# Row sums of a softmax: from the exponential's accumulator to a column of ones beside the values

## The reference

```python
x = x + attn(layernorm(x));  x = x + ffn(layernorm(x))

# attn, B=4, S=1024, D=128
scores = einsum('bqe,bke->bqk', x @ W_qk, x) * D**-0.5 + (kpos - qpos) * slope
attn   = softmax(where(qpos >= kpos, scores, -inf), axis=-1)
out    = einsum('bqk,bkd->bqd', attn, x @ W_v.T)

# ffn, HIDDEN=384, weights int32 / 127
out = (silu(x @ wg.T) * (x @ wu.T)) @ wd.T
```

## Time and profile before

| | us |
|---|---|
| median of 3 runs | 144.62 |
| lowest and highest run | 144.57, 145.28 |
| the profiled execution's own time | 145.67 |
| its span, first to last instruction | 143.9 |
| opening (weights, first projections), up to about | 24 |
| four rounds of attention, up to about | 104 |
| FFN, up to the end | 143.9 |

### The profile page before, as it was taken

The page is one execution under the profiler, slowest core; times in us unless marked ns, Lnnn a source line. Parts: engine busy times, 40 slices in busy tenths (PEclk is TensorE's granted clock), DMA queues, the critical chain, the costliest instruction groups (busy, mean ns, idle before and its releaser), DMA issues.

```text
span 143.9 us, 3450 instructions
## 1 busy us (share of the span) xinstructions
PE 122.8 (85%) x1215; PEld 91.9 (64%) x1215; DVE 120.7 (84%) x341; ACT 110.7 (77%) x251; POOL 97.6 (68%) x157
## 2 busy tenths in 40 slices
PE   0239658999999999999999998979998899999942
PEld 0028345867987769978779776657755656675541
DVE  0729989998697996969996969999879999988781
ACT  4034588999976999949999769985699978999830
POOL 6490769964993454992438943798999999646810
PEclk9999999999999999999999999999999999999995
DMA  4997000000000000000000000000000222022204
GB/s 129 221 244 190 0 0 2 7 2 0 5 0 0 5 0 2 5 0 0 0 5 0 5 0 2 2 5 0 5 0 0 77 77 66 12 73 77 77 0 146
DMA packets 9811, 5.18 MB, mean 36 GB/s; under 512 B 448, under 2 KB 9792, under 8 KB 9792
## 3 DMA queue, kind: packets, MB, share of 16 engines
q1 hardware_dynamic: 9792, 4.92, 12.2%
HBM read 2.82 MB, written 2.10 MB: 34 GB/s over the span
## 4 chain that ended last, share of the span: by engine, by line
PE 50%; DVE 23%; ACT 9%; POOL 7%; DMA 4%; issue 3%; SPq 2%; DVEq 0%
PE work_ps L556 7%; POOL hidden_lo L411 6%; PE attn_ps L571 5%; PE attn_ps L573 4%; PE attn_ps L572 4%; PE score_ps L504 4%; PE score_ps L506 4%; DVE probsT_lo L824 4%; PE score_ps L505 4%; DMA wd_int<-in_L_ffn_w_down_dram 4%; DVE biased L841 3%; PE score_ps L595 2%; PE score_ps L592 2%; DVE stats L726 2%; ACT silu L1069 2%
## 5 line engine op out<-in xcount | busy, mean ns | idle before, releaser
L571 PE MATMUL attn_ps<-v_hi,probsT_hi 128*128 128x128 f16 x144 | 25.8, 219 | 3.0 <-DVE xs L851 2.4
L824 DVE TENSOR_TENSOR probsT_lo<-work_ps,probsT_hi 128x512 f16<-128x512 f32 (+3 forms) x48 | 25.2, 552 | 3.5 <-ACT probsT_hi L1007 3.4
L1007 ACT CAST probsT_hi<-work_ps 128x512 f16<-128x512 f32 (+3 forms) x48 | 21.4, 484 | 7.7 <-PE work_ps L556 7.4
L992 ACT ACTIVATE probs<-biased,neg_max 128x128 f32<-128x128 f32 (+7 forms) x32 | 25.0, 783 | 1.9 <-DVE neg_max L841 1.9
L841 DVE CUSTOM_DVE_ANT_0 biased<-score_ps,bias,neg_score_scale 128x128 f32<-128x128 f32 (+7 forms) x32 | 25.8, 806 | 0.6 <-PE score_ps L506 0.6
L573 PE MATMUL attn_ps<-v_hi,probsT_lo 128*128 128x128 f16 x144 | 25.8, 219 | 0.0
L572 PE MATMUL attn_ps<-v_lo,probsT_hi 128*128 128x128 f16 x144 | 25.8, 219 | 0.0
L556 PE MATMUL work_ps<-ident,probs 128*128 128x128 f32 x144 | 21.4, 274 | 0.2 <-DVE probsT_lo L824 0.2
L411 POOL TENSOR_TENSOR hidden_lo<-hidden,hidden_hi 128x512 f16<-128x512 f32 x13 | 17.6, 1375 | 5.1 <-ACT hidden_hi L1075 5.1
L556 PEld LDWEIGHTS work_ps<-ident,probs 128*128 128x128 f32 x144 | 16.5, 141 | 3.2 <-DVE probsT_lo L824 0.5
L437 POOL TENSOR_TENSOR xT_lo<-whole,xT_hi 128x512 f16<-128x512 f32 x8 | 9.3, 1163 | 13.6 <-ACT whole L986 13.6
(11 more groups left out here) (135 smaller groups left out, 346.7 us busy)
## 6 DMA issues: line engine op xcount, KB each, us to landing
out_dram<-xs SPq DMA_DIRECT2D x7, 256.0 KB, 2.7
xs<-in_L_attn_x_dram SPq DMA_DIRECT2D x3, 512.0 KB, 7.4
xs<-in_L_attn_x_dram SPq DMA_DIRECT2D x2, 256.0 KB, 3.0
out_dram<-xs SPq DMA_DIRECT2D x2, 128.0 KB, 1.9
wgu_int<-in_L_ffn_w_gate_dram SPq DMA_DIRECT2D x1, 192.0 KB, 3.1
wgu_int<-in_L_ffn_w_up_dram SPq DMA_DIRECT2D x1, 192.0 KB, 3.4
wd_int<-in_L_ffn_w_down_dram SPq DMA_DIRECT2D x1, 192.0 KB, 5.1
wqk_in<-in_L_attn_W_qk_dram SPq DMA_DIRECT2D x1, 64.0 KB, 2.9
```

The costliest lines, as they stand in the source:

```text
L571: pe.matmul(attn_ps[:, 0:D], p_hi, v_j, start=(j == 0), stop=False)
L824: dve.tensor_tensor(probsT_lo[:, i % 2, cols], work_ps[:, bank, 0:n], probsT_hi[:, i % 2, cols], ALU.subtract).then_inc(work_emptied, 1)
L992: act.activation(probs[:, i % 2, 0:n], biased[:, i % 2, 0:n], ACT.Exp, bias=neg_max[:, i:i + 1], scale=-1.0, accum_out=prob_sum[:, i:i + 1 ...
L1007: act.copy(probsT_hi[:, i % 2, CW * h:CW * h + n], work_ps[:, bank, 0:n]).then_inc(probsT_hi_ready, 1)
```

## The change

What it does, part by part (line numbers of the changed kernel are lower by some 35 to 40):

- The exponential has no `accum_out`. `scale_sum`, with its instruction on ScalarE for every tile, is gone, and so is `prob_sum`.
- The values' high half is laid out as eight tiles of 136 columns (`VW = D + 8`), of which column 128 holds 1.0. GpSimd writes these ones once in the opening; TensorE waits for `v_ones_ready` once.
- In `weigh_values` the two products with the values' high half have 129 columns, so that column 128 of `attn_ps` becomes the sum of the row's probabilities, high and low part. The product with the values' low half keeps 128.
- VectorE multiplies that column by `wpow_inv` (a `tensor_scalar` from PSUM), inverts it and adds, all in `add_attention`. Each of the three waits for the semaphore of the one before, and the first for `attn_ready`. The reciprocal at the head of a tile is gone; its waits for scores and probabilities now stand before `bias_scores`.
- `place`, `emptied`, `copied_before` and their like are replaced by one list, `ring`, of everything that goes through `work_ps` in order; it gives the same banks and the same counts. Tests of the kind `isinstance(b, int)` go.

```diff
-        prob_sum = sb("prob_sum", [P, TB], F32)
-        v_hi = sb("v_hi", [P, 2, S], F16)
-        v_lo = sb("v_lo", [P, 2, S], F16)
+        VW = D + 8
+        v_hi = sb("v_hi", [P, 2, TB, VW], F16)
+        v_lo = sb("v_lo", [P, 2, TB, D], F16)
...
+            pool.memset(v_hi[:, :, :, D:D + 1], 1.0).then_inc(v_ones_ready, 1)
             pool.wait_ge(const_ready, N_CONST)
...
             def weigh_values(b, par, i):
...
                 pe.wait_ge(attn_added, TB * b + i)
                 for j in range(i + 1):
                     keys = slice(P * j, P * (j + 1))
                     p_hi, p_lo = probsT_hi[:, i % 2, keys], probsT_lo[:, i % 2, keys]
-                    v_j = at(v_hi, par, keys)
-                    pe.matmul(attn_ps[:, 0:D], p_hi, v_j, start=(j == 0), stop=False)
-                    pe.matmul(attn_ps[:, 0:D], p_hi, at(v_lo, par, keys), start=False, stop=False)
-                    m = pe.matmul(attn_ps[:, 0:D], p_lo, v_j, start=False, stop=(j == i))
+                    v_j = v_hi[:, par, j, 0:D + 1]
+                    pe.matmul(attn_ps[:, 0:D + 1], p_hi, v_j, start=(j == 0), stop=False)
+                    pe.matmul(attn_ps[:, 0:D], p_hi, v_lo[:, par, j, :], start=False, stop=False)
+                    m = pe.matmul(attn_ps[:, 0:D + 1], p_lo, v_j, start=False, stop=(j == i))
                 m.then_inc(attn_ready, 1)
...
-            def inverse_sum(b, i, more):
-
+            def inverse_sum(b, i):
                 t = TB * b + i
+                dve.wait_ge(attn_ready, t + 1)
+                dve.tensor_scalar(scaled_sum[:, i:i + 1], attn_ps[:, D:D + 1], wpow_inv[:, 1:2], None, ALU.mult)\
+                   .then_inc(scaled_ready, 1)
                 dve.wait_ge(scaled_ready, t + 1)
-                if more:
-
-
-                    dve.wait_ge(probs_ready, t + 2)
-                    dve.wait_ge(scores_ready, t + 4)
                 dve.reciprocal(inv_sum[:, i:i + 1], scaled_sum[:, i:i + 1]).then_inc(inv_ready, 1)
...
             def add_attention(b, i):
                 t = TB * b + i
+                inverse_sum(b, i)
                 dve.wait_ge(inv_ready, t + 1)
-                dve.wait_ge(attn_ready, t + 1)
...
             def around(b, par, nxt, final):
                 for i in range(TB):
                     more = i + 3 < TB or not final
-                    inverse_sum(b, i, more)
                     if more:
+
+                        dve.wait_ge(scores_ready, TB * b + i + 4)
+                        dve.wait_ge(probs_ready, TB * b + i + 2)
                         bias_scores((i + 3) % TB)
...
+                if kind == "v":
+                    act.copy(hi[:, par, CT * h:CT * h + CT, 0:D], work_ps[:, bank, :].rearrange("p (t d) -> p t d", d=D))\
+                       .then_inc(hi_ready, 1)
+                    return
...
                 act.activation(probs[:, i % 2, 0:n], biased[:, i % 2, 0:n], ACT.Exp, bias=neg_max[:, i:i + 1],
-                               scale=-1.0, accum_out=prob_sum[:, i:i + 1]).then_inc(probs_ready, 1)
-
-            def scale_sum(b, i):
-
-                t = TB * b + i
-                act.wait_ge(probs_ready, t + 1)
-                act.activation(scaled_sum[:, i:i + 1], prob_sum[:, i:i + 1], ACT.Copy, scale=wpow_inv[:, 1:2])\
-                   .then_inc(scaled_ready, 1)
+                               scale=-1.0).then_inc(probs_ready, 1)
```

More of the change, by code:

```diff
@@ L66, in preln_block @@
[L66 to L103, removed]
+    def parts_at(b, i):
+        return prologue[:HALVES if b == B - 1 else None][i - 1:i] if i else []
+    ring = [(kind, 0, h) for kind, h in prologue] + [("P", 0, 0, 0)]
@@ new lines, in preln_block, with bank_of, filled, by_pool @@
+    for b in range(B):
+        for i in range(TB):
+            nb, ni = (b, i + 1) if i + 1 < TB else (b + 1, 0)
+            if nb < B:
+                ring += [("P", nb, ni, h) for h in range(ni // CT + 1)]
+            ring += [(kind, b + 1, h) for kind, h in parts_at(b, i)]
+    ring_index = {key: n for n, key in enumerate(ring)}
+    def bank_of(key):
+        return ring_index[key] % NWORK
+    def filled(key):
+        return ring_index[key] + 1
+    def by_pool(key):
+        return key[0] in ("xT", "q") and key[1] > 0
@@ L105, in at, with emptied @@
+    def emptied(key):
+        return sum(by_pool(k) == by_pool(key) for k in ring[:ring_index[key] + 1])
+    VECTOR_TAKES, POOL_TAKES = (sum(by_pool(k) == who for k in ring) for who in (False, True))
     def at(buffer, half, columns):
-        if isinstance(half, int):
-            return buffer[:, half, columns]
-        return buffer[:, ds(half, 1), columns].rearrange("p a n -> p (a n)")
+        return buffer[:, half, columns]
     with ExitStack() as ctx:
@@ L441, in _ @@
                 nxt = (b + 1) % 2
-                for part in prologue:
-                    if by_pool(part):
-                        split_low(b + 1, nxt, *part)
+                for kind, h in prologue:
+                    if by_pool((kind, b + 1, h)):
+                        split_low(b + 1, nxt, kind, h)
                 norm(b + 2)
@@ L538, in scores @@
                 if i in (0, 2):
-                    taken(b - 1, ("q", i // 2))
-                if not (isinstance(t, int) and t < 2):
+                    taken(("q", b, i // 2))
+                if t >= 2:
                     pe.wait_ge(biased_ready, t - 1)
@@ L872, in around @@
                         split_probsT(b + 1, 0)
-                    for part in parts_at(i, final):
-                        if not by_pool(part):
+                    for part in parts_at(b, i):
+                        if not by_pool((part[0], b + 1, part[1])):
                             split_low(b + 1, nxt, *part)
```

121 lines of the change are left out of this document (54 added, 67 removed).

## The result

| | kernel before | changed kernel |
|---|---|---|
| median of the runs, us | 144.59 (4 runs) | 150.75 (4 runs, 150.09 to 152.03) |
| ratio, 95% interval | | 1.042 [1.038, 1.047] |
| profiled execution: time, span | 145.67, 143.9 | 151.21, 149.4 |

The forecast was 150.2 us, in a range of 147.0 to 153.5. The two profiled executions differ by 5.5 us, the medians by 6.2.

What follows compares the result with a forecast made beforehand. No engine alone was taken as the bound; middle rounds run through VectorE's work, then TensorE's last weighing, and VectorE bounds the last round's start. 3.6 + 1.9 + 0.1 = 5.6 us on 144.62 gave 150.2 us, range 147.0 to 153.5.

Steps and rivals of the forecast that it cites:

- The price of a tile: VectorE ahead of each addition: waited scaling 0.25 plus reciprocal 0.20, less the old 0.07, 0.38 us more per tile.
- A middle round: Seven tiles' 2.66 us first fill 1.50 us of VectorE idle; with 0.04 from the eighth, 1.20 us longer.
- ScalarE's part, costed at nothing: ScalarE loses 0.28 us of work per tile, 9 us over 32 tiles; predicted to gain no time.
- Rival 1: ScalarE's relief pays and a tile costs VectorE only 0.07 us: faster, 142.1 us; chance 6%.
- 4 x 0.28: Relief over four tiles brings ScalarE's copy at 77.46 earlier by 1.1 us, in the faster case.
- Round one: First attention round, counted among the three rounds that each get 1.20 us longer.
- The last round: No idle to fill before the weighing at 97.43: five tiles at 0.38, 1.9 us longer.
- I add nothing for them: Chains behind the last round's weighing at 97.43 run beside TensorE's weighings and FFN products: 0 us added.
- The sum: Whole kernel: 3.6 + 1.9 + 0.1 = 5.6 us slower, giving 150.2 us.
- Rival 2: VectorE's slack exceeds its gaps or the scaling is shorter, 0.21 to 0.30 us a tile: 145.8 to 148 us; 8%.
- Rival 3: Work banks: TensorE starts tile 6's transposes 1.0 us late, ScalarE's copy may follow late: 151.7 to 153.2 us; 13%.
- Rival 4: Weighing's products: 129 columns cost as much as 256, 15 us more, 160 us or so; 3%.

Runs made afterwards that it cites:

- e5: Kernel before plus the two waited small VectorE operations at each tile's head, beside the old reciprocal, results unused: 151.69 us, ratio 1.048.
- e10: Kernel before plus two more reciprocals at each tile's head that wait for nothing and that nothing waits for: 145.63 us, ratio 1.007.
- e3: Changed kernel with ScalarE's accumulator read and its scaling of the sums kept, into an unused column: 152.79 us, ratio 1.048.
- e6: Kernel before without ScalarE's accumulator read and sum scaling, VectorE's reciprocal reading a constant: 143.81 us, ratio 0.993.
- e7: Changed kernel without scaling and reciprocal for the last round's last three tiles, which use tile 4's inverse: 149.96 us, ratio 1.035 to the kernel before.
- e1: Kernel before with the column of ones, 129-column products and padded values, sums still from the accumulator: 144.73 us, ratio 1.001.
- e8: Changed kernel run again unaltered, on the same chip as e7: 151.63 us, ratio 1.042 to the kernel before.
- e2: Kernel before plus a waited scaling and a waited reciprocal on VectorE ahead of each addition, results unused: 151.91 us, ratio 1.047.
- e4: Changed kernel with the power of two written in the added column, so VectorE's scaling goes and its reciprocal reads PSUM: 145.61 us, ratio 1.005.
- e9: Kernel before with value weights not divided by their power of two, so the accumulated sums need no scaling: 144.01 us, ratio 0.995.

## Why the prediction was right

**The price of a tile** was the step that carried it. Taken: 0.25 + 0.20 - 0.07 = 0.38 us. Measured: 0.24 + 0.20 - 0.07 = 0.37. That a waited small operation costs 0.20 us and more, and an unwaited one 0.07, was read from the earlier trace rows and holds in e5 and e10. The Trainium skill, VectorE: DVE Perf Modes, section The DRAIN you can't avoid, has it, from eight copies in a row, that a semaphore between two VectorE operations costs nothing extra, though also that a next operation which is not held starts earlier. For reciprocals of one element a row these two runs show a wait to cost: 0.07 us without one, 0.20 with one.

**A middle round.** Taken: 7 x 0.38 - 1.50 + 0.04 = 1.20 us. Measured 1.15. The parts agree as well: five chains ahead of the split, 5 x 0.37 = 1.85 us, meet 0.33 + 0.32 + 1.18 = 1.83 us of idle, and the stretch stayed the same within 0.1 us (13.64 against 13.73). The closeness is in part luck, for two small errors cancel here: 0.13 us of the last gap was not filled, and VectorE came to the split only 0.96 us later (13.51 against 12.55 us into the round) where 1.85 us of chains less 0.65 of idle make 1.20, so that some 0.2 us was hidden by something that no gap shows. Behind it the chains of tiles 5 and 6 add 2 x 0.37 = 0.74, that of tile 7 its whole 0.44 and the wait for the last weighing 0.10: 1.28, measured 1.24. e5 is the test of this reading, since it moves the chains from behind the split to ahead of it, with the sum as computed.

**ScalarE's part, costed at nothing.** Right as a term, and e3 sizes it: 0.14 us a round, a wait that the change would otherwise have kept. Rival 1, in which the relief pays, fell on both of its legs: a waited operation is not worth 0.07 us, and the relief alone (e6) shortens a round by 0.27 us and not by 1.0; the step "4 x 0.28" should have been 1 x 0.28, since ScalarE waits for TensorE ahead of the copy of tile 5.

**Round one** was counted as a middle round, 1.20 us. From the start of its first weighing to that of its last it took 18.75 us instead of 18.07: 0.68, a term sized too large by 0.5; its gaps before (0.40 and 1.18 us) do not explain this, and it stays open.

**The last round.** Taken: 5 x 0.38 = 1.9 us up to the weighing that starts at 97.43. It now starts at 101.74, 16.95 us behind the one of tile 7 before it (84.79), against 15.29 (82.14 to 97.43): 1.66 us.

**The step that failed** is "I add nothing for them", for the chains behind that weighing. The part from there to the end grew by 1.19 us. From the weighing of tile 5 to the last addition it is 7.09 us instead of 6.39, two or three chains, and the last statistics stand behind that addition. GpSimd's rows, changed kernel, then before:

```profile
107.05 2.04 POOL L359 TENSOR_TENSOR centred<-xs,mean 128x512 f32<-128x512 f32 x2
109.59 0.21 POOL L334 TENSOR_TENSOR mean_sum<-stats 128x8 f32<-128x8 f32 x1 [0.50 <-DVE stats L687]
```

```profile
102.80 2.04 POOL L386 TENSOR_TENSOR centred<-xs,mean 128x512 f32<-128x512 f32 x2
104.80 0.21 POOL L361 TENSOR_TENSOR mean_sum<-stats 128x8 f32<-128x8 f32 x1
```

Before, GpSimd went on to the second layer norm's last moments without a pause; now it waits 0.50 us for VectorE, and the first FFN stages wait for what follows. The first FFN addition comes 0.32 us later behind the weighing of tile 5 (101.74 to 115.62 against 97.43 to 110.99), and the next interval between FFN additions is 4.69 us where it was 4.09: 0.9 us together. e7 shows the size from the other side: without those three chains the kernel is 1.0 us faster at full clock. The other 0.28 of the 1.19 us lies behind the start of the last big FFN addition (138.82 to 143.9 against 144.04 to 149.4). There TensorE's clock fell to half in both profiles, 0.9 us behind that start in the kernel before (139.7) and 0.6 us in the changed one (144.6), so this part need not be the chains'.

**The sum.** 5.5 us between the profiled executions, 5.6 predicted. Read at the starts of the weighings, the tail's 1.2 us too little was made up by round one (0.5 too much), the last round (0.2), the two middle rounds and the columns (0.1 each), and an opening that was 0.3 us shorter in the profiled execution (a DMA landed at 8.57 us and not at 8.93). Part of the closeness is errors that cancel: with the tail's term put right and the others as they stood, the forecast would have been 151.4 us, still inside the range.

**Rivals 2 to 4.** Rival 2 (more slack than the gaps show): e5 uses up the 1.50 us to the last tenth and no more; 0.2 us of such slack shows in the changed kernel and in e10, too little for the rival's 145.8 to 148 us. Rival 3 (the work banks) was to show as TensorE starting transposes late and VectorE then waiting for the copy. The first half came: in each middle round TensorE waits 0.50 us for the bank and starts tile 6's transposes 0.61 us late (1.0 had been worked out). The second half hardly did. The copy came at 13.02 us into the round against 13.11 before, for ScalarE, relieved, had less in front of it, and VectorE stood 0.13 us for it. This path is nearly as long as VectorE's own. Rival 4 (the odd column) fell with e1.

## What to carry to other kernels

A sum that comes for little from another engine's accumulator is not made cheaper by a free column in a matrix product, if the engine that must finish it is the one that sets the end: price the handful of tiny operations by their count and by whether each waits for the one before it. Fill the measured gaps in order, with the work that stands ahead of each; what stood behind the last gap of a round was paid in full here. And a wait names the engine that came last: ask what that engine was itself waiting for, before relieving it.

## What the runs showed of the hardware

**TensorE's clock.** In some executions of the changed kernel the granted clock fell from full speed (2.4 GHz) to half (1.2 GHz) in the middle of the last round. Busy time of TensorE by stretch of 1 us, second profile of the changed kernel (e8; columns: the stretch, its length, TensorE's busy us and count, its granted clock, DMA's share, GB/s):

```profile
100.00:101.00 1.00, 0.00 (x0) 1.00 0.00 0
101.00:102.00 1.00, 0.49 (x9) 1.00 0.00 0
102.00:103.00 1.00, 1.00 (x14) 0.58 0.06 16
103.00:104.00 1.00, 1.00 (x7) 0.50 0.00 0
104.00:105.00 1.00, 1.00 (x6) 0.50 0.00 0
105.00:106.00 1.00, 1.00 (x6) 0.72 0.00 0
106.00:107.00 1.00, 1.00 (x21) 1.00 0.00 0
```

Ahead of it TensorE had idled, and its products of tile 5 came after that; its rows, first of e8 and then of the first profile of the same kernel:

```profile
101.51 0.22 PE L531 MATMUL attn_ps<-v_hi,probsT_hi 128*128 128x129 f16 x1 [1.55 <-DVE xs L815]
...
102.85 1.91 PE L518 MATMUL work_ps<-ident,probs 128*128 128x128 f32 x8
```

```profile
101.74 0.22 PE L531 MATMUL attn_ps<-v_hi,probsT_hi 128*128 128x129 f16 x1 [1.55 <-DVE xs L815]
...
102.75 1.04 PE L518 MATMUL work_ps<-ident,probs 128*128 128x128 f32 x8
```

The same idle of 1.55 us, and once the clock fell, once it did not: eight transposes took 1.91 or 1.04 us, and the last addition started 1.4 us later in the one profile (110.26 against 108.83) though the weighing had started 0.2 us earlier. Of the ten timed executions of the changed kernel three had a mean clock of 0.976 and took 152.0 to 152.7 us; one at 0.983 took 152.17, those at 1.0 took 150.05 to 150.27. In the kernels with two waited operations added (the changed one, e2, e3, e5, e7), 9 of 31 executions (the disturbed one left out) had a mean clock of 0.977 or less; in the kernel before (53 that ran beside the experiments), e1, e4, e6, e9 and e10, none of 104 was under 0.981. So some of the median's 6.2 us, against 5.6 at full clock (150.1 to 144.5), is a second cost of the change.

Its cause was not tested. A longer idle of TensorE ahead of tile 5's products is one candidate: it is 1.55 us in the profiles of the changed kernel, e2, e3, e7 and e8, of which e3, e7 and e8 show the drop there. Against its length alone stands that in e5 it is 1.10 us, as in the kernel before, and one of e5's six executions still had a clock of 0.974, while e4 has 1.30 us and no such execution in ten.

**Small operations** on VectorE, all of 128x1, one element a row: a reciprocal took 0.07 us start to start with nothing waiting for it and 0.20 us when the next operation did, a scaling that the next waits for 0.24 us. Other sizes were not tried.
